# Gate of the attention layer: inner layer by row on GpSimd in three bf16 parts, second layer as one stacked bf16 pass

## The reference

```python
q, k = rope(bf16(x @ Wq.T)), rope(bf16(x @ Wk.T))
o = where(causal, exp(q @ k.T / 16), 0).sum(-1)          # one number per position
g = relu(o[..., None] @ fc1_w.T + fc1_b) @ fc2_w.T + fc2_b   # 1 -> 16 -> 256
x1 = layernorm(x + g)
# mixture of experts, 12 experts, the 3 best of each row by x1 @ (U P_w).T
h = gelu(sum_e C1[:, e] * (x1 @ W1[e].T))
y = sum_e C2[:, e] * (h @ W2[e].T) + C3 @ b2
return layernorm(x1 + y)
```

## Time and profile before

| | us |
|---|---|
| median of 3 runs (311.31 to 315.37) | 312.19 |
| profiled execution, its own time | 311.88 |
| its span | 310.0 |
| PE busy | 273.9 (88%) |
| DVE busy | 249.2 (80%) |
| ACT busy | 164.0 (53%) |
| POOL busy | 145.2 (47%) |
| L808 (second layer), 64 matmul records in 16 calls of `fc`, summed busy | 19.3 |
| L782 (gate transposes), 32 records, summed busy | 4.8 |
| L577 (relu), 8 records, summed busy | 6.1 |

### The profile page before, as it was taken

How to read it: one execution, slowest core, us unless ns; L and a number is a source line. 1 busy time by engine, 2 the same in 40 slices (tenths; PEclk the granted TensorE clock), 3 DMA queues, 4 the chain that set the end, 5 groups by cost and what they waited for, 6 DMA issues and landing times.

```text
span 310.0 us, 6417 instructions
## 1 busy us (share of the span) xinstructions
PE 273.9 (88%) x2028; PEld 196.9 (64%) x2030; DVE 249.2 (80%) x728; ACT 164.0 (53%) x341; POOL 145.2 (47%) x315
## 2 busy tenths in 40 slices
PE   7997999979791985999998998998998999899980
PEld 5443455434351553778887787787777878688870
DVE  0378689999979265488999999999999989987872
ACT  1247746755662116406854854854854956654430
POOL 0200017999999611225356256256256353374421
PEclk9999999997998598699999999999999999999997
DMA  8998999950000000000010010011000010110111
GB/s 235 416 393 246 169 169 207 146 71 0 0 3 1 0 0 0 2 2 19 19 30 23 18 30 26 17 27 30 18 24 30 20 32 26 32 32 21 37 34 38
DMA packets 19211, 20.50 MB, mean 66 GB/s; under 512 B 1620, under 2 KB 18408, under 8 KB 18664
## 3 DMA queue, kind: packets, MB, share of 16 engines
q1 hardware_dynamic: 18456, 19.13, 26.2%
q10 hardware_dynamic: 720, 0.93, 1.0%
HBM read 15.83 MB, written 4.19 MB: 65 GB/s over the span
## 4 chain that ended last, share of the span: by engine, by line
PE 40%; DVE 27%; POOL 14%; issue 8%; SPq 4%; DMA 4%; ACT 2%; DVEq 0%; POOLq 0%
PE bank L922 31%; DVE early L1287 9%; POOL W L406 5%; DMA W<-in_w2T 4%; POOL wtmp L403 4%; POOL W L405 3%; PE bank L760 2%; PE bank L808 2%; DVE early L1336 2%; SPq L333 2%; DVE st L1331 2%; DVE top L1156 2%; DVE x1T L1146 1%; DVE stats L1135 1%; DVE zrest L1171 1%
## 5 line engine op out<-in xcount | busy, mean ns | idle before, releaser
L922 PE MATMUL bank<-W,x1T 128*128 (+1 forms) x630 | 79.4, 281 | 8.5 <-DVE early L1287 5.0
L922 PE MATMUL bank<-W,early 128*128 (+1 forms) x630 | 74.5, 273 | 6.0 <-DVE early L1336 5.4
L922 PEld LDWEIGHTS bank<-W,x1T 128*128 128x128 f16 x630 | 61.4, 101 | 21.9 <-DVE early L1287 7.2
L1287 DVE SCALAR_TENSOR_TENSOR early<-bank,Csel,early 128x256 f32<-128x256 f32 x124 | 59.7, 482 | 14.2 <-PE bank L922 9.7
L922 PEld LDWEIGHTS bank<-W,early 128*128 128x128 f16 x630 | 59.5, 98 | 17.4 <-DVE early L1336 7.0
L760 PE MATMUL bank<-early,wqk 128*128 128x512 f32 x128 | 61.3, 611 | 2.4 <-ACT qk L551 1.8
L760 PEld LDWEIGHTS bank<-early,wqk 128*128 128x128 f32 x128 | 22.6, 193 | 22.9 <-issue 20.3
L672 ACT ACTIVATE early<-early 128x256 f32<-128x256 f32 x32 | 13.3, 417 | 45.0 <-DVE early L1287 44.7
L509 POOL TENSOR_SCALAR ve<-mv 128x1 f32<-128x1 f32 x32 | 7.3, 228 | 59.6 <-DVE mv L1332 58.9
L551 ACT ACTIVATE qk<-bank 128x512 bf16<-128x512 f32 x32 | 18.9, 594 | 30.6 <-PE bank L760 30.4
L1062 DVE TENSOR_TENSOR xcos<-qk,cb 128x1024 bf16<-128x1024 bf16 x16 | 12.0, 749 | 18.6 <-ACT qk L551 18.5
(11 more groups left out here) (117 smaller groups left out, 454.5 us busy)
## 6 DMA issues: line engine op xcount, KB each, us to landing
early<-in_xT SPq DMA_DIRECT2D x16, 256.0 KB, 7.8
xs<-in_x SPq DMA_DIRECT2D x32, 128.0 KB, 7.9
out<-early SPq DMA_DIRECT2D x32, 128.0 KB
W<-in_w1T SPq DMA_DIRECT2D x1, 2048.0 KB, 11.8
W<-in_w2T SPq DMA_DIRECT2D x1, 2048.0 KB, 12.4
W<-in_w1T SPq DMA_DIRECT2D x1, 1024.0 KB, 7.2
W<-in_w2T SPq DMA_DIRECT2D x1, 1024.0 KB, 14.1
wqk<-in_wqkT ACTq DMA_DIRECT2D x1, 512.0 KB, 3.7
```

The lines of the kernel that those rows point to most:

```text
L922: mm = pe.matmul(where[:, 0:DIM], lhs(hx, c), w, start=(k == 0), stop=(k == 5))
L1287: dve.scalar_tensor_tensor(sums, bank[place[n]][:, 0:DIM], c, before, ALU.mult, ALU.add)\
```

## The change

`fc1`'s weight and bias rows are spread over all partitions once, by a small fp32 matmul (`gate_rows`, after the first projection of chunk 1) and a DVE copy (`gate_spread`). `o` keeps all four stripes. The inner layer of a stripe is made in rows by seven dependent GpSimd operations on 8 x 17 = 136 elements of each partition (`gate_parts`; two of them write 408 and 272). Their result, six parts of 17 as bf16, is transposed with eight bf16 transposes per stripe (four fp32 ones per chunk before) and copied by ACT (`gate_copy`, 102 partitions by 1024 bf16, four in all). `fc` becomes a single bf16 matmul per tile with K = 102. `fc2` is loaded as 17 rows, split on GpSimd and copied to its six places by DMA. The relu calls, and the wait of `exps` on the transposes, go. In chunk 3 the places of `fc(0, 0)` and of its add move behind `project(3, 1)` and `rope(3, 0)`.

```diff
+        GATE = (4, 4, 6, 6)
@@ SP
             load_chunk(1)
+            sp.dma_start(fc2f[:, :], fc2[0:NI, :]).then_inc(ld_rows, 16)
...
             load_chunk(3)
-            sp.dma_start(fc2s[:, :], fc2).then_inc(ld_rows, 16)
+            sp.wait_ge(fc2_split, 1)
             sp.wait_ge(b2_split, 1)
             for k in range(NP):
+                sp.dma_start(fc2s[NI * k:NI * (k + 1), :], fc2p[:, RIGHT[k], :]).then_inc(fc2_spread, 16)
                 sp.dma_start(b2s[NE * k:NE * (k + 1), :], b2p[:, RIGHT[k], :]).then_inc(b2_spread, 16)
@@ POOL
+            def gate_parts(T):
+                pool.wait_ge(exp_done, NSEQ * (T + 1))
+                wait(pool, hgT_done, T)
+                if T == 0:
+                    pool.wait_ge(gwb_done, 1)
+                w, b = (gwb[:, n, :].unsqueeze(1).to_broadcast([P, NSEQ, NI]) for n in range(2))
+                f = hg[:, :, :].unsqueeze(2)
+                link(pool.tensor_tensor(hg[:, :, :], o[:, T, :].unsqueeze(2).to_broadcast([P, NSEQ, NI]), w, ALU.mult))
+                link(pool.tensor_tensor(hg[:, :, :], hg[:, :, :], b, ALU.add))
+                link(pool.tensor_scalar(hg[:, :, :], hg[:, :, :], 0.0, 0.0, ALU.max, ALU.add))
+                link(pool.tensor_copy(hgp[:, :, 0:3, :], f.to_broadcast([P, NSEQ, 3, NI])))
+                link(pool.tensor_tensor(hg[:, :, :], hg[:, :, :], hgp[:, :, 0, :], ALU.subtract))
+                link(pool.tensor_copy(hgp[:, :, 3:5, :], f.to_broadcast([P, NSEQ, 2, NI])))
+                pool.tensor_tensor(hgp[:, :, 5, :], hg[:, :, :], hgp[:, :, 3, :], ALU.subtract).then_inc(hgp_done, 1)
...
             def aux(k, s, pos):
+                if (k, s, pos) == (1, 0, 0):
+                    gate_parts(3)
...
             for c in range(NCH):
                 for j in range(4):
                     early_aux(c, j, early)
+                    if (c, j) in ((2, 3), (5, 0)):
+                        gate_parts(c // 4)
                     if c >= 4:
                         w_piece(piece)
                         piece += 1
             select_of(0)
             C3_split(0)
-
+            gate_parts(2)
             norm_scale(2)
@@ ACT
-            def gate_relu(c):
...
+            def gate_copy(T):
+                act.wait_ge(hgT_done, T + 1)
+                act.activation(hgT[0:NP * NI, T, :, :, :].rearrange("p u s r -> p s u r"),
+                               bank[GATE[T]][0:NP * NI, :].bitcast(BF16).rearrange("p (s u r) -> p s u r", s=NSEQ, r=RPS),
+                               ACT.Copy).then_inc(hgT_copied, 1)
...
             def aux(k, s, pos):
+                if (s, pos) == (2, 0) and k in (0, 1):
+                    gate_copy(k + 2)
...
                 qk_copy(c, 0)
+                if c in (3, 6):
+                    gate_copy(c // 6)
                 qk_copy(c, 1)
@@ PE
+            def gate_transpose(T):
+                pe.wait_ge(hgp_done, T + 1)
+                wait(pe, hgT_copied, T)
+                if T >= 2:
+                    pe.wait_ge(x1lo_done, begun["x1T"])
+                    wait(pe, C3T_copied, begun["C3T"])
...
+                for b in range(NSEQ):
+                    tr = pe.transpose(spread[:, b * P:(b + 1) * P], hgp[:, b, :, :].rearrange("p k i -> p (k i)"),
+                                      const(C_IDENT, P))
                 tr.then_inc(hgT_done, 1)
...
-                    mm = pe.matmul(bank[ROWS][:, t % 2 * DIM:(t % 2 + 1) * DIM], hgT[PAD * T:PAD * (T + 1), u, :, :].rearrange("p b r -> p (b r)"),
-                              fc2s[PAD * T:PAD * (T + 1), :], start=True, stop=True)
+                    mm = pe.matmul(bank[ROWS][:, t % 2 * DIM:(t % 2 + 1) * DIM], hgT[0:NP * NI, T, u, :, :].rearrange("p b r -> p (b r)"),
+                                   fc2s[:, :], start=True, stop=True)
...
             for c in range(NCH):
                 project(c, 0)
-                early_aux(c, 0, early)
+                if c == 1:
+                    gate_rows()
+                if c in (3, 6):
+                    gate_transpose(c // 6)
+                if c != 3:
+                    early_aux(c, 0, early)
                 project(c, 1)
+                if c == 3:
+                    early_aux(c, 0, early)
...
                 early_aux(c, 3, early)
-                if c:
-                    gate_transpose(c - 1)
@@ DVE
                 early_aux(c, 0, early)
-                early_aux(c, 1, early)
+                if c != 3:
+                    early_aux(c, 1, early)
...
                 rope(c, 0)
+                if c == 1:
+                    gate_spread()
+                if c == 3:
+                    early_aux(c, 1, early)
```

More of the change, by code:

```diff
@@ L554, in exps @@
             def exps(c, part):
-                T = c // 2
-                if part == 0:
-                    wait(act, hgT_done, c - 1)
+                T, b = c // 2, SPC * (c % 2)
                 for s in (2 * part, 2 * part + 1):
@@ L776, in scores, with gate_rows @@
                               start=False, stop=True, skip_group_check=True).then_inc(score_done, 1)
-            def gate_transpose(c):
-                pe.wait_ge(exp_done, SPC * (c + 1))
-                wait(pe, hgT_copied, c)
-                for s in range(SPC):
-                    tr = pe.transpose(bank[HGT][0:PAD, P * s:P * (s + 1)],
-                                      o[:, c % 2, s:s + 1].to_broadcast([P, PAD]), identf[:, :])
-                tr.then_inc(hgT_done, 1)
+            def gate_transpose(T):
[4 more added lines that the diff above has]
+                    wait(pe, C3T_copied, begun["C3T"])
+                begun["gate"] += 1
+                spread = bank[GATE[T]][0:NP * NI, :].bitcast(BF16)
+                for b in range(NSEQ):
+                    tr = pe.transpose(spread[:, b * P:(b + 1) * P], hgp[:, b, :, :].rearrange("p k i -> p (k i)"),
+                                      const(C_IDENT, P))
+                tr.then_inc(hgT_done, 1)
+            def gate_rows():
+                pe.wait_ge(amax_done, 1)
+                pe.wait_ge(grow_done, 1)
+                pe.matmul(bank[MISC][:, 0:2 * NI], onesg[:, :], grow[:, :, :].rearrange("p n i -> p (n i)"),
+                          start=True, stop=True).then_inc(grow_spread, 1)
             def peak_transpose():
@@ L792, in peak_spread @@
                 pe.matmul(bank[MISC][:, P:P + 3], ones3[:, :], diag[:, :], start=True, stop=True).then_inc(bcast_done, 1)
-            begun = {"fc": 0, "bias": 0, "x1T": 0, "C3T": 0, "logits": 0, "count": 0}
+            begun = {"gate": 0, "fc": 0, "bias": 0, "x1T": 0, "C3T": 0, "logits": 0, "count": 0}
             def fc(g, h):
@@ L815, in x1_transpose @@
                 wait(pe, C3T_copied, begun["C3T"])
+                wait(pe, hgT_copied, begun["gate"])
                 begun["x1T"] += 1
@@ L886, in aux @@
             def aux(k, s, pos):
+                if (s, pos) == (2, 0) and k in (0, 1):
+                    gate_transpose(k + 2)
                 if (s, pos) == (0, 0):
@@ L988, in _ @@
             first(range(7, NE))
-            gate_transpose(NCH - 1)
             aux(0, 0, 0)
```

55 lines of the change are left out of this document (37 added, 18 removed).

## The result

The changed kernel takes 318.8 us in the median of four runs (317.74 to 320.70), against 311.93 for the one before: ratio 1.021, 95% interval 1.015 to 1.027. On a second chip the same kernel took 318.52 against 312.70, 1.017 (1.010 to 1.024). The forecast was 313.4 us, and its range ended at 318.5: the time lies just outside, on the slow side, and the likeliest case, a change too small to tell, did not come.

A forecast was written before the change was run, and what follows sets the result against it. Bound by stage: DMA, projections and DVE's search, then POOL's weight split to 89.5 us, PE from 101 to 117, DVE in the loop. L429 +4.2, then -2.4, -0.5, +0.2: +1.5 on 311.88, so 313.4 us, range 309.5 to 318.5.

The forecast's parts named there:

- term 3: Chunk 3: PE waits for `gate_parts(0)` and DVE's rotation runs beside POOL, delaying the scales; +1.0 us, bounds 0 and 3.
- terms 2 and 4: POOL's weight split: +4.1 us for `gate_parts(1)`; -0.9 us because the last two pieces before L429 run without DVE beside them.
- term 1: PE work saved, 0.83 us per `fc` call: -2.4 us from 101 to 117 us, -0.5 in the loop.
- at nothing: Side effects priced at about nothing; among them `gate_transpose(2)`, about 0.2 us net on PE, +0.7 at a bad time.
- Term 2: `gate_parts(1)` in the POOL chain ahead of L429 costs its own length: +4.1 us, bounds 3.0 and 7.
- PE's saving is worth more than POOL's work: Loop gives back 0.83 us for each of five calls, `gate_parts` takes 3.0 us: 308.1 us; chance 0.22 for 306 to 311.5.
- GpSimd is the new bound: POOL chain: `gate_parts` takes 7 us or more, L429 moves by 9.1; +6.2 to +9.2, 318 to 321 us; chance 0.11.

The follow-up runs named there:

- the POOL operations alone: Kernel before plus the seven `gate_parts` operations at the change's four places, on scratch data nobody reads: 316.48 us, ratio 1.013.
- the run with one POOL operation: Changed kernel with one GpSimd operation per stripe in place of the seven: 1308.19 us, because the program ran its fallback over all experts.
- the five-fold `fc`: Changed kernel with each matmul of the second layer issued five times, so `fc` holds PE as long as before: 318.83 us, ratio 1.018.
- the fillers of chunk 3: Changed kernel with twenty matmuls on zeros on PE ahead of its wait for stripe 0 in chunk 3: 315.52 us, ratio 1.011.
- the last kernel of the experiments: Changed kernel, three waits moved, last eight weight pieces late (three ahead of `norm_scale(2)`, behind `gate_parts(2)`; five after it), ten zero matmuls at 29 us: 310.08 us, 0.996.
- stripe 0 later: Changed kernel with stripe 0's transpose (now behind `peak_transpose`), copy and two `fc` calls one to two steps later in chunk 3: 314.36 us, ratio 1.007.
- all three moved: Changed kernel with stripe 0's transpose later, stripe 1's parts behind `C3_split(0)`, stripe 2's transpose ahead of `bias(0, 0)`: 312.74 us, ratio 0.998.

## Why the prediction was wrong

| step | foreseen, us | in the two traces, us |
|---|---|---|
| term 3, chunk 3 | +1.0 (0 to 3) | +4.5 |
| terms 2 and 4, `gate_parts(1)` less relief | +3.2 | +3.8 |
| term 1, stage 101 to 117 us | -2.4 | -3.2 |
| at nothing: `gate_transpose(2)` | +0.2 (+0.7) | +4.0 |
| term 1, the loop | -0.5 (0 to -4.2) | -0.2 |
| sum | +1.5 | +8.9 |

**Term 2 was right in mechanism and within its bounds.** 4.1 us foreseen for `gate_parts(1)`, 4.83 measured (seven operations and their hand-overs), and the POOL operations alone, in the kernel before, make L429 late by 4.66 and the kernel slower by 3.8. The prediction's own factor of 1.23 on 3.6 would have given 4.4, nearer than the 4.1 that it took. The parts of the sum were less good: the scalar operation on 136 elements, priced at 0.33 us, takes 0.68 alone, and the cast of 408, priced at 0.52, takes 0.54.

**Term 1 was right in both halves, less so in its parts.** 3.2 us in its stage (3.7 in the run with one POOL operation) and none in the loop. From the product ahead of `fc(2, 0)` to `logits` there are 16.27 us before, 13.06 after and 14.50 with the five-fold `fc`. So the two calls of `fc` give 1.4 of the 3.2, where 2.0 were foreseen, and 1.8 come with `fc` as long as before, where 0.4 were foreseen for the transpose; the rest of these was not told apart. The rival in which "PE's saving is worth more than POOL's work" is refuted by the five-fold `fc`: 0.3 us for the whole second layer.

**Term 3 failed.** The prediction foresaw the pause of 1.5 to 2.5 us, and priced it as if PE went on behind it at its old pace: `project(3, 1)` "is over at 39.3". The 4.5 fall in two. With both projections at their full pace (the fillers of chunk 3) the split starts at 50.15, so 1.8 us are late without the clock. DVE beside POOL is 0.8 of these, from POOL's operations alone. The pause itself is only 0.3 of them: the last kernel of the experiments has no such pause, a clock of 1.00 over 20 to 48 us, and its split at 49.82. The rest, some 0.7, isn't told apart; `project(2, 2)` was late by 0.44 before chunk 3 began. The two slow projections are the other 2.7, of which `project(3, 1)` is 1.4 (3.32 against 1.94) and `project(2, 2)` up to 1.6 (3.55 against 1.99), the latter not steadily the change's. So the bounds of 0 to 3 held all but the clock, and the clock was in none of them. The rule that the prediction cites (the Trainium skill, SBUF — State Buffer, "SBUF: two separate sides") gave 1.2 to 2.1 us by the prediction's estimate for the part that it speaks of, DVE beside POOL; the 0.76 of the trace lies under that, and of a PE that waits the rule says nothing.

**"At nothing" failed on `gate_transpose(2)`.** The text named its wait, for DVE's low part of group 2, and put it at 0.2, or 0.7 "if the transpose comes at a bad time". It is a pause of 1.87 us directly ahead of the twelve products, and these took 10.26 us where 8.4 had been. Moving that one call is worth 4.1 us in the medians, and it stood in a clause. But of the 4.0 us in the traces only 0.8 are the place's own, since with the same wait and the clock up behind it (stripe 0 later) the stage takes 23.31 us against 22.54; the other 3.2 are the clock. The error is the same as in term 3: a wait on PE was priced by its length, at the full clock for all that follows.

**Taken together.** In ratios, as microseconds of 312, POOL's work costs 4.0 (1.013), stripe 2's place 4.4 (1.017 to 1.003) and the pause in chunk 3 some 2.1 (1.017 to 1.011); `logits` gains 3.2 to 3.7. That is 4.0 + 4.4 + 2.1 - 3.5 = +7.0, against +6.7 and +5.4 measured (1.021 and 1.017). The terms come from two chips and overlap: moving stripe 0 alone gave back, in its trace, 3.2 us of what is counted here for stripe 2. So this is a rough sum and no proof. What is shown is that the order at these three places is the loss, since with all three moved the time is level with before.

**The rivals.** The one on the other side, "GpSimd is the new bound", gave 318 to 321 us, and the time fell there, but not by its mechanism: its condition, a `gate_parts` of 7 us or more, was not met (4.7 and 4.83). That the number came out there is luck. It belongs to a case that the prediction didn't have: a new PE wait can cost the clock of what follows as well.

## What to carry to other kernels

A new wait on PE is to be priced as a range: at most its length if the clock holds, and as the upper end its length plus what the matmuls behind it lose at the lower clock. Here the same wait of 1.87 us cost 0.8 us in one kernel and 4.0 in another. So a small operation that another engine feeds belongs in a pause that PE has anyway, and the first thing to look for is that pause. And before an engine's chain is lengthened or relieved, read what stands in it: eight weight pieces that nobody was waiting for were worth 9 us, more than anything in the change.

## What the runs showed of the hardware that was not expected

- The granted clock of a run tells its time, in one and the same kernel. Of 52 runs of the kernel before, those with a mean of 0.965 or 0.966 took 310.8 to 312.0 us, those with 0.948 to 0.953 took 314.8 to 316.7. A ratio of two kernels within 1% needs many runs of each.
- The same 72 products behind the same wait of 1.87 us took 8.03 us in one trace and 10.19 to 10.26 in three. In the first the granted clock was back at 132.2 us, in the changed kernel only at 142.3; the fall itself, at 125.2 to 125.4, lies ahead of the wait in both.
- Four fp32 matmuls behind a pause of 2.1 to 2.6 us took 3.14 to 3.37 us in six traces. Behind the same pause (2.62 us) they took 1.94 where ten matmuls on zeros had shortened the pause at 29 us, 8 us ahead of it.
- A GpSimd scalar operation with two immediates on 136 fp32 elements took 0.68 us, as long as one on 512 elements with a scale from memory (0.69); a cast that writes 408 elements took 0.54.
- Beside the DVE rotations, operations of GpSimd that take 0.44 and 0.54 us alone took 0.74 and 0.96 (36.02 to 37.80 us in the changed kernel).
